# Two-layer cross-attention: layer norms in one operation, weights applied when leaving PSUM, score shift for 512 queries at once

## The chip, the cores and the metric

The kernel runs on one core of one Trainium2 chip. The metric is device time in microseconds (us) from the program's start to its end. A core has TensorE (PE in the profile, with PEld for its weight loads), VectorE (DVE), ScalarE (ACT), GpSimd (POOL) and SyncE (SP, which here only issues DMAs). They run side by side and wait for each other by semaphores. SBUF is the working memory, PSUM takes what PE computes.

## What is computed

Two batches of 512 queries (256 wide) attend to 1024 context tokens (192 wide), in two layers. In layer 0 both sides are normalised, with weights and shifts; layer 1 has eight heads, no norm in front, and ends in a norm. The norms that are changed are those of layer 0, the first of the two; layer 1's final norm is as it was.

```python
def layer_norm(x, gamma, beta):
    mu = jnp.mean(x, axis=-1, keepdims=True)
    var = jnp.mean(jnp.square(x - mu), axis=-1, keepdims=True)
    return (x - mu) * jax.lax.rsqrt(var + EPS) * gamma + beta
# layer 0
qn, kvn = layer_norm(q_feat, g_q, be_q), layer_norm(kv_feat, g_kv, be_kv)
q = qn @ Wq.T + bq ; k = kvn @ Wk.T + bk ; v = kvn @ Wv.T + bv
ctx = softmax(q @ k.T) @ v
x = q_feat + ctx @ Wd.T + bd
# layer 1: Q, K, V for 8 heads of 256, softmax(Q K^T / 16) V, @ Wo, + x, layer norm
```

## The kernel before

All matmuls take rounded fp32 operands (fp32r); each operand is split in a rounded part ("hi", written by ACT) and the remainder ("lo", written by DVE or POOL), so a product takes two or three matmuls. The weights Wq and Wk are multiplied with each other once (`absorb`, tasks T_A0 and T_A0b), so a query tile is multiplied with raw keys; likewise Wv and Wd (T_B0, T_B0b). Bias terms become two small vectors (`vec`, task T_VEC) and, for each query, one number that is added to its scores (`neg_shift`). Before softmax, DVE adds it and takes the row's minimum of the negated scores (`minimum(-1, j, 0)`, L1352), for one tile j of 128 queries after another. There is one score buffer, `ps_scores`, so PE's `scores(-1, j+1)` waits for `minimum(-1, j)`.

Every engine runs its own hand-written list of instructions in order, and that order decides everything: an instruction that waits holds all that stand behind it on its engine.

The norm of a 128-token tile went in four steps. DVE took statistics (L1470, L1478, L1481); POOL made `rstd` from the variances (L431); DVE subtracted the mean and multiplied by gamma (`ln_centre`, L1492); then, for query tiles and half of the context tiles, ACT multiplied by `rstd` (L1127) and POOL added beta (L440), and for the other half DVE did both (`ln_scale_context`, L1501). PE then transposed the tiles (`turn_chunk`, L779: two chunks of the queries, four of the context), ACT rounded them (`round_chunk`, L1142) and DVE took the remainders (`split_chunk`). The shift of the scores was a sum over each query row on DVE (`sum_shift`, L1529, four operations per batch, and `finish_shift`, L1538); its weights came from a matmul at PE's start (L792). Batch 0 goes through at once; batch 1's norm stands between batch 0's softmax steps.

Batch 0's values (`values(-1, 0, c)`, c = 0 to 3, L650 to L658) run from 46.79 us, with batch 1's context chunks turned between c = 2 and c = 3. Behind them comes `scores(-1, 4)`, the first of batch 1.

## Time and profile before

| | us |
|---|---|
| median of 3 runs (501.72 to 502.06) | 501.74 |
| the profiled execution | 501.67 |
| its span in the profile | 499.7 |
| outside the span | 1.97 |
| PE busy | 474.2 (95%) |
| DVE busy | 332.2 (66%) |
| ACT busy | 291.6 (58%) |
| POOL busy | 245.4 (49%) |

A share is the mean over stages with different limits. A row of the timeline gives start and duration; matmuls overlap, so PE's pace is the distance between their starts. The change is only in what runs in the first 60 us and in the form of the loads and stores.

### The profile page before, as it was taken

What the parts mean: (1) busy time and instruction counts of PE and PEld (TensorE: products, weight loads), DVE (VectorE), ACT (ScalarE), POOL (GpSimd) and SP (SyncE); (2) the same over time, 40 slices, a digit from 0 to 9 for tenths busy, and PEclk for the clock granted to TensorE, in tenths of its full rate; (3) what the DMA queues carried; (4) which work ended last, traced back from release to release, by engine and by line L of the source; (5) the groups of instructions that cost most, each with busy time, mean ns of one, the idle gap of its engine ahead of it and who ended that gap; (6) DMA issues with size and microseconds to landing.
All of it is one profiled execution on the core that took longest, in us unless ns stands there. A gap on an engine that the chain in (4) does not pass through costs nothing.

```text
span 499.7 us, 7565 instructions
## 1 busy us (share of the span) xinstructions
PE 474.2 (95%) x2424; PEld 395.8 (79%) x2424; DVE 332.2 (66%) x679; ACT 291.6 (58%) x482; POOL 245.4 (49%) x153
## 2 busy tenths in 40 slices
PE   0999999999999999999999999999999999999994
PEld 0877787787878888888888888888888888888893
DVE  4999866476685657565856585658565765673666
ACT  4667476467664756566666665656565655556332
POOL 4636763555855353637272717172727263454004
PEclk9999999999999999999999999999999999999998
DMA  8413013667765565665656564647473746562002
GB/s 263 147 45 127 1 29 120 212 206 227 246 214 182 177 202 176 205 211 168 210 168 210 168 214 164 226 153 238 140 244 135 252 137 220 168 210 64 0 2 84
DMA packets 53975, 81.97 MB, mean 164 GB/s; under 512 B 5793, under 2 KB 43073, under 8 KB 53825
## 3 DMA queue, kind: packets, MB, share of 16 engines
q1 hardware_dynamic: 44992, 50.16, 33.8%
q10 hardware_dynamic: 8960, 31.54, 16.8%
q8 instruction: 11, 0.18, 0.2%
q14 instruction: 12, 0.09, 0.1%
HBM read 49.16 MB, written 32.51 MB: 163 GB/s over the span
## 4 chain that ended last, share of the span: by engine, by line
PE 74%; DVE 8%; DMA 7%; ACT 4%; issue 3%; POOL 2%; SPq 1%; DVEq 0%; POOLq 0%; ACTq 0%
PE ps_scores L626 27%; PE ps_o L658 6%; PE ps_o L651 5%; PE ps_o L650 5%; PE ps_o L657 5%; PE ps_o L652 5%; DMA scratch<-probs 3%; PE ps_task L574 2%; PE ps_task L573 2%; PE ps_task L572 2%; DMA probs_t_lo<-scratch 2%; DMA ring<-in_weights_a 2%; PE ps_out L572 2%; PE ps_out L573 1%; PE ps_out L574 1%
## 5 line engine op out<-in xcount | busy, mean ns | idle before, releaser
L514 POOL TENSOR_TENSOR probs_t_lo<-probs_t_lo,probs_t_hi 128x1024 fp32r<-128x1024 f32 (+1 forms) x75 | 146.5, 1967 | 177.5 <-ACT probs_t_hi L1018 177.4
L1018 ACT ACTIVATE probs_t_hi<-probs_t_lo 128x1024 fp32r<-128x1024 f32 (+1 forms) x75 | 64.7, 881 | 37.2 <-DMA probs_t_lo<-scratch 34.7
L626 PE MATMUL ps_scores<-key_hi,q_hi 128*128 128x512 f32 x144 | 57.8, 402 | 1.3 <-DVE neg_scores L1352 0.8
L1339 DVE RECIPROCAL row_inv<-row_sum 128x1 f32<-128x1 f32 x72 | 11.3, 159 | 70.4 <-PE ps_scores L626 68.4
L650 PE MATMUL ps_o<-probs_t_hi,val_hi 128*128 128x512 f32 (+1 forms) x144 | 56.7, 393 | 1.1 <-issue 0.9
L626 PE MATMUL ps_scores<-key_rem,q_lo 128*128 128x512 f32 x144 | 56.6, 393 | 0.5 <-DVE q_lo L1434 0.3
L626 PE MATMUL ps_scores<-key_rem,q_hi 128*128 128x512 f32 x144 | 56.6, 393 | 0.0
L626 PE MATMUL ps_scores<-key_lo,q_hi 128*128 128x512 f32 x144 | 56.6, 393 | 0.0
L626 PE MATMUL ps_scores<-key_hi,q_lo 128*128 128x512 f32 x144 | 56.4, 392 | 0.0
L651 PE MATMUL ps_o<-probs_t_lo,val_hi 128*128 128x512 f32 (+1 forms) x144 | 56.3, 391 | 0.0
L658 PE MATMUL ps_o<-probs_t_lo,val_rem 128*128 128x512 f32 (+1 forms) x144 | 56.2, 392 | 0.0
L657 PE MATMUL ps_o<-probs_t_hi,val_rem 128*128 128x512 f32 (+1 forms) x144 | 55.8, 389 | 0.0
L652 PE MATMUL ps_o<-probs_t_hi,val_lo 128*128 128x512 f32 (+1 forms) x144 | 55.6, 386 | 0.0
L1376 DVE STREAM_TRANSPOSE probs<-probs 128x1024 f32<-128x1024 f32 x30 | 37.4, 1246 | 25.0 <-ACT probs L1006 24.8
L1376 DVE STREAM_TRANSPOSE neg_scores<-neg_scores 128x1024 f32<-128x1024 f32 x30 | 37.3, 1242 | 15.1 <-ACT neg_scores L1006 15.1
L444 POOL TENSOR_TENSOR w_lo<-ring,w_hi 128x1024 fp32r<-128x1024 f32 x17 | 40.9, 2408 | 6.2 <-ACT w_hi L1098 6.2
L1006 ACT ACTIVATE neg_scores<-neg_scores,row_min 128x1024 f32<-128x1024 f32 x30 | 34.5, 1148 | 13.1 <-DVE row_min L1369 13.1
L1369 DVE CUSTOM_DVE_ANT_0 probs<-ps_scores,mask_bias 128x1024 f32<-128x1024 f32 x32 | 38.9, 1216 | 3.2 <-PE ps_scores L626 3.2
L1006 ACT ACTIVATE probs<-probs,row_min 128x1024 f32<-128x1024 f32 x30 | 34.5, 1151 | 11.1 <-DVE row_min L1369 11.0
L1369 DVE CUSTOM_DVE_ANT_0 neg_scores<-ps_scores,mask_bias 128x1024 f32<-128x1024 f32 x32 | 38.8, 1213 | 0.6 <-issue 0.6
L626 PEld LDWEIGHTS ps_scores<-key_hi,q_hi 128*128 128x128 f32 x144 | 27.0, 188 | 7.5 <-DVE neg_scores L1352 2.2
L626 PEld LDWEIGHTS ps_scores<-key_rem,q_lo 128*128 128x128 f32 x144 | 27.0, 188 | 7.2 <-DVE q_lo L1434 0.6
(256 smaller groups left out, 1097.5 us busy)
## 6 DMA issues: line engine op xcount, KB each, us to landing
probs_t_lo<-scratch SPq DMA_DIRECT2D x240, 128.0 KB, 2.9
scratch<-neg_scores ACTq DMA_DIRECT2D x30, 512.0 KB, 3.1
scratch<-probs ACTq DMA_DIRECT2D x30, 512.0 KB, 3.7
ring<-in_weights_a SPq DMA_DIRECT2D x9, 512.0 KB, 5.2
ring<-in_weights_b SPq DMA_DIRECT2D x9, 512.0 KB, 5.1
ring<-in_keys_t SPq DMA_DIRECT2D x4, 512.0 KB, 3.2
ctx_raw<-in_context SPq DMA_DIRECT2D x2, 768.0 KB, 9.5
ring<-in_context SPq DMA_DIRECT2D x16, 96.0 KB, 2.6
```

Of the source, the lines that this page charges most:

```text
L444: nc.gpsimd.tensor_tensor(w_lo[:, :], ring[r][:, :], w_hi[:, :].bitcast(f32), ALU.subtract)\
L514: nc.gpsimd.tensor_tensor(pt_lo[b][:, t, k, :], pt_lo[b][:, t, k, :].bitcast(f32), moved_part(j, k).bitcast(f32), ALU.subtract).then_inc(m ...
L626: last = pe.matmul(ps_scores[:, n], left, right[:, n], start=(i == 0), stop=(i == len(passes) - 1))
L650: pe.matmul(o0, val_hi[b][:, kt, :], hi, start=(kt == 0), stop=False)
L651: pe.matmul(l0, val_hi[b][:, kt, :], lo, start=False, stop=False)
L652: pe.matmul(o0, val_lo[b][:, kt, :], hi, start=False, stop=(kt == KT - 1))
L657: pe.matmul(o1, val_rem[b][:, kt, :], hi, start=(kt == 0), stop=False)
L658: last = pe.matmul(l1, val_rem[b][:, kt, :], lo, start=False, stop=(kt == KT - 1))
L1006: act.activation(dst, src, ACT.Exp, bias=row_min[:, j:j + 1], scale=-1.0, accum_out=row_sum[:, j:j + 1]).then_inc(exped, 1)
L1018: act.activation(moved_part(j, k), pt_lo[b][:, t, k, :].bitcast(f32), ACT.Copy)\
L1369: dve.tensor_tensor_reduce(out=tiles[j % 2][:, :], in0=ps_scores[:, :], in1=mask_bias[:, b, :], scale=1.0, scalar=BIG, op0=ALU.add, op1=AL ...
L1376: dve.transpose(tiles[j % 2][:, :], tiles[j % 2][:, :]).then_inc(blocks_turned, 1)
```

## The change

- **Loads.** A partition now holds 4 neighbouring query tokens (8 context tokens) instead of every 128th, so each partition reads or writes one piece. Context of batch 0 comes in two transfers. The rows of gamma are no longer spread over 128 partitions by DMA: they come as one row each on ACT's queue and PE turns them into columns (`gains`).
- **Norm.** One operation makes `(x - mean) * rstd`: on ACT as `rstd * x + neg_means` (queries and the first context half), on DVE as a tensor_scalar (second half). DVE makes `neg_means` (`shift_means`) from POOL's `rstd`. `rsqrt` is three operations of 4 columns per batch's start instead of one of 4 and one of 8. `ln_centre`, `ln_scale_context`, `scale_tiles`, `bias_tiles` are gone.
- **Weights.** Gamma is the scale of what already leaves PSUM (`round_chunk`, `split_chunk`, `round_b`, `split_b0`).
- **Shifts.** Beta times the weight matrices is added to the biases by DVE: `fold_bias`, two sums over a row (L1575) and an addition, for bq, bk and bv.
- **Score shift.** PE multiplies the two columns `w_pair` with all 512 transposed queries (four matmuls), ACT copies the two rows out (`keep_shift`), PE turns them (`turn_shift`), DVE adds up.
- **Order.** The T_VEC matmuls stand behind all six chunks.

```diff
-            sp.dma_start(resid[:, 0:QT, :], x_tiles[:, 0:QT, :]).then_inc(x_loaded[0], 16)
-            sp.dma_start(q_rows[:, :, :], rows_q.partition_broadcast(P)).then_inc(q_rows_loaded, 16)
-            sp.dma_start(ctx_raw[:, 0:KT, :], ctx_tiles[:, 0:KT, :]).then_inc(ctx_loaded[0], 16)
-            sp.dma_start(kv_rows[:, :, :], rows_kv.partition_broadcast(P)).then_inc(kv_rows_loaded, 16)
+            sp.dma_start(resid[:, 0:QT, :], x_tiles[0]).then_inc(x_loaded[0], 16)
+            sp.dma_start(ctx_raw[:, 0:CTX_HALF, :], ctx_tiles[0, :, 0:CTX_HALF, :]).then_inc(ctx_loaded[0], 16)
+            sp.dma_start(ctx_raw[:, CTX_HALF:KT, :], ctx_tiles[0, :, CTX_HALF:KT, :]).then_inc(ctx_loaded[1], 16)
             sp.dma_start(ring[0][:, :], weights_a[0]).then_inc(ring_loaded[0], 16)
+            sp.dma_start(be_row[:, :], rows_q[1].partition_broadcast(P)).then_inc(be_row_loaded, 16)
+            sp.dma_start(kv_row[:, :], rows_kv[1].partition_broadcast(P)).then_inc(kv_row_loaded, 16)
...
+            def sum_shift(b, bank):
+                for k in range(DT):
+                    mv = slice(b * QUERIES, (b + 1) * QUERIES)
+                    pe.matmul(bank[0:2, :], w_pair[:, k, :], xt_hi[:, k, mv], start=(k == 0), stop=False)
+                    last = pe.matmul(bank[0:2, :], w_pair[:, k, :], xt_lo[:, k, mv], start=False, stop=(k == DT - 1))
+                last.then_inc(shift_rowed, 1)
...
+            def norm_tokens(b):
+                act.wait_ge(means_made, 2 * b + 1)
+                for t in range(KT, LN_TILES):
+                    n, x_tile = b * LN_TILES + t, b * QT + t - KT
+                    act.activation(xn[:, x_tile, :], resid[:, x_tile, :], ACT.Identity,
+                                   scale=rstd[:, n:n + 1], bias=neg_means[:, n:n + 1]).then_inc(x_normed, 1)
...
+            def shift_means(b, first, end, rstds):
+                n = slice(b * LN_TILES + first, b * LN_TILES + end)
+                dve.wait_ge(rstd_made, 3 * b + rstds)
+                dve.scalar_tensor_tensor(neg_means[:, n], moments[:, n, 0], -1.0, rstd[:, n], ALU.mult, ALU.mult)\
+                    .then_inc(means_made, 1)
...
             split_queries(T_Q0, 0, 0, 0)
             split_queries(T_Q0b, 0, 1, 0)
-            sum_shift(0, range(QT))
-            finish_shift(0)
+            split_chunk(0, 4)
+            split_chunk(0, 5)
+            finish_shift(0, w_bank[:, 0:2 * QT])
+            dve.wait_ge(ring_loaded[1], 16)
+            fold_bias(C_BV, ring[1], 0, kv_row, bias_v_folded)
             minimum(-1, 0, 0)
             ln_stats(1, x_token_tiles, x_loaded[1])
             ln_moments(1, KT, LN_TILES)
+            shift_means(1, KT, LN_TILES, 1)
             split_b0(T_B0, 0)
             split_b0(T_B0b, 1)
...
-            ln_centre(1, x_token_tiles)
             split_probs(-1, 0)
```

DVE between the remainders of batch 0's queries (`q_lo`) and the second minimum. Before (L1529 is the old score shift, L1352 the minimum, L1423 `split_b0`):

```order
L1434 SCALAR_TENSOR_TENSOR q_lo<-ps_task,vec,q_hi 64x512
L1529 ISA ctx_raw,neg_shift<-xn,rem_sum 128x2x128
L1529 ISA neg_shift 128x1
L1538 TENSOR_SCALAR neg_shift<-neg_shift,vec 128x4
L1352 TENSOR_SCALAR neg_scores,row_min<-ps_scores,neg_shift 128x1024
L1470 BN_STATS stats<-resid 128x6 x4
L1478 BN_AGGR moments<-stats 128x2 x4
L1481 TENSOR_SCALAR var_eps<-moments 128x4
L1423 TENSOR_TENSOR b_lo<-ps_out,b_hi 128x256
```

The same place in the changed kernel, behind the same `q_lo` row (L1505) and one more `split_chunk` row (L1600). L1603 is `split_chunk`, L1613 to L1617 `finish_shift`, L1575 and L1579 `fold_bias` for bv, L1422 the minimum, L1566 `shift_means`; `split_b0` (L1493) follows:

```order
L1603 SCALAR_TENSOR_TENSOR key_rem<-ps_turn,gains,key_rem 64x512
L1613 TENSOR_SCALAR vec<-ps_turn 128x1
L1614 TENSOR_SCALAR shift_parts<-ps_turn 128x4
L1617 SCALAR_TENSOR_TENSOR neg_shift<-shift_parts,vec,ps_turn 128x4
L1575 ISA probs,bias_parts<-ring,kv_row 128x192
L1575 ISA bias_parts 128x1
L1579 TENSOR_TENSOR bias_cols<-bias_parts,cols 128x2
L1422 TENSOR_SCALAR neg_scores,row_min<-ps_scores,neg_shift 128x1024
L1541 BN_STATS stats<-resid 128x6 x4
L1549 BN_AGGR moments<-stats 128x2 x4
L1552 TENSOR_SCALAR var_eps<-moments 128x4
L1566 SCALAR_TENSOR_TENSOR neg_means<-moments,rstd 128x4
```

Two chunk remainders and the fold of bv now stand ahead of the first minimum, and `shift_means`, which waits for POOL's `rstd`, ahead of `split_b0` and the second; the four old sums are gone. The pair of rows L1529 stands four times in the program before, the pair L1575 twice here; each is shown once.

PE from the last product of Wq and Wk to the queries. Before (L803 is T_VEC, L779 the transposes of chunks):

```order
L574 MATMUL ps_out<-w_hi,w_lo 128x256
L803 MATMUL ps_o<-cols,ring 128x1 x4
L803 MATMUL ps_o<-cols,b_full 128x1 x2
L779 MATMUL ps_scores<-ident,kvn 128x128 x4
L779 MATMUL ps_o<-ident,kvn 128x128 x4
L779 MATMUL ps_scores<-ident,kvn 128x128 x4
L779 MATMUL ps_o<-ident,kvn 128x128 x4
L572 MATMUL ps_out<-xt_hi,a_hi 128x512
```

In the changed kernel:

```order
L793 MATMUL ps_turn<-ident,kvn 128x128 x4
L840 MATMUL ps_o<-bias_cols,ring 128x1 x4
L844 MATMUL ps_o<-bias_cols,ring 128x1 x4
L800 MATMUL ps_turn<-xt_hi,w_pair 2x512
L801 MATMUL ps_turn<-xt_lo,w_pair 2x512
L800 MATMUL ps_turn<-xt_hi,w_pair 2x512
L801 MATMUL ps_turn<-xt_lo,w_pair 2x512
L584 MATMUL ps_out<-xt_hi,a_hi 128x512
```

T_VEC moved behind the chunks, and directly behind it, with only DVE's short `split_w` between, PE needs `w_pair`.

PE in batch 0's values, at c = 0 and 1 of the changed kernel (L664 to L672 are the values; before, no foreign row stands here):

```order
L672 MATMUL ps_o<-probs_t_lo,val_rem 128x512
L800 MATMUL ps_task<-xt_hi,w_pair 2x512
L801 MATMUL ps_task<-xt_lo,w_pair 2x512
L800 MATMUL ps_task<-xt_hi,w_pair 2x512
L801 MATMUL ps_task<-xt_lo,w_pair 2x512
L664 MATMUL ps_o<-probs_t_hi,val_hi 128x512
```

Four matmuls are added here, and four small transposes (L812) after c = 1.

## Rows read from the trace of the kernel before

**Rows 1.** Windows: stretch and length, busy us (instructions) of each engine, granted clock, DMA

```profile
15.00:20.00 5.00, 4.79 (x35) 4.55 (x33) 5.00 (x15) 3.71 (x10) 3.84 (x5) 1.00 0.35 101
30.00:40.00 10.00, 9.21 (x50) 7.29 (x49) 9.41 (x27) 8.60 (x18) 6.17 (x6) 1.00 0.16 53
33.10:43.60 10.50, 9.30 (x50) 7.29 (x50) 9.97 (x24) 10.41 (x20) 8.29 (x7) 1.00 0.40 142
40.00:50.00 10.00, 8.80 (x48) 6.75 (x46) 9.55 (x31) 6.73 (x14) 5.55 (x5) 1.00 0.41 158
50.00:60.00 10.00, 9.51 (x48) 7.19 (x47) 9.20 (x21) 4.57 (x11) 9.67 (x12) 1.00 0.01 2
100.00:450.00 350.00, 348.17 (x1718) 290.47 (x1717) 228.56 (x413) 213.06 (x335) 178.52 (x90) 1.00 0.61 195
```

**Rows 2.** Timeline, DVE at the start: start, us, engine, line, operation, tiles, count

```profile
4.72 1.41 DVE L1470 BATCH_NORM_STATS2 stats<-resid 128x6 f32<-128x256 f32 x4 [4.72 <-DMA resid<-in_x]
6.45 0.17 DVE L1481 TENSOR_SCALAR var_eps<-moments 128x4 f32<-128x4 f32 x1
...
12.74 1.23 DVE L1556 TENSOR_TENSOR w_lo<-ring,w_hi 128x1024 fp32r<-128x1024 f32 x1
13.88 2.71 DVE L1492 SCALAR_TENSOR_TENSOR kvn<-ctx_raw,moments,kv_rows 128x192 f32<-128x192 f32 x8
...
17.83 1.28 DVE L1509 TENSOR_TENSOR xt_lo<-ps_turn,xt_hi 128x512 fp32r<-128x512 f32 x2
...
31.35 0.22 DVE L1584 TENSOR_SCALAR mask_bias<-mask_bias 16x128 f32<-16x128 f32 x1
```

**Rows 3.** Timeline, ACT and POOL, same columns

```profile
7.82 1.71 ACT L1127 ACTIVATE xn<-xn,rstd 128x256 f32<-128x256 f32 x4 [1.16 <-POOL rstd L431]
22.95 2.39 POOL L444 TENSOR_TENSOR w_lo<-ring,w_hi 128x1024 fp32r<-128x1024 f32 x1 [2.93 <-ACT w_hi L1098]
30.37 1.02 POOL L431 TENSOR_TENSOR rstd<-var_eps,minus_half 128x4 f32<-128x4 f32 x1 [5.03 <-DVE var_eps L1481]
```

**Rows 4.** Timeline, PE from its first transposes to the first scores

```profile
13.60 1.91 PE L779 MATMUL ps_turn<-ident,xn 128*128 128x128 f32 x8
...
15.16 0.56 PE L572 MATMUL ps_task<-w_hi 128*128 128x256 f32 x1
...
16.99 0.28 PE L574 MATMUL ps_out<-w_hi,w_lo 128*128 128x256 f32 x1
...
20.94 0.48 PE L572 MATMUL ps_out<-xt_hi,a_hi 128*128 128x512 f32 x1
...
23.75 0.40 PE L626 MATMUL ps_scores<-key_hi,q_hi 128*128 128x512 f32 x1
```

**Rows 5.** Timeline, DVE from the last query remainder to the second minimum

```profile
24.68 0.74 DVE L1434 SCALAR_TENSOR_TENSOR q_lo<-ps_task,vec,q_hi 64x512 fp32r<-64x512 f32 x1 [0.36 <-ACT q_hi L1075]
...
26.38 0.41 DVE L1529 CUSTOM_DVE_ANT_0 ctx_raw<-xn,rem_sum 128x256 f32<-128x256 f32 x1
26.72 0.07 DVE L1529 DVE_READ_ACCUMULATOR2_ANT neg_shift<- 128x1 f32 x1
26.83 0.23 DVE L1538 TENSOR_SCALAR neg_shift<-neg_shift,vec 128x4 f32<-128x4 f32 x1
27.20 1.28 DVE L1352 TENSOR_SCALAR_CACHE_REDUCE neg_scores<-ps_scores,neg_shift 128x1024 f32<-128x1024 f32 x1
...
31.67 1.28 DVE L1352 TENSOR_SCALAR_CACHE_REDUCE neg_scores<-ps_scores,neg_shift 128x1024 f32<-128x1024 f32 x1
```

**Rows 6.** Timeline, PE at the second scores, and in batch 0's values

```profile
28.54 0.50 PE L626 MATMUL ps_scores<-key_hi,q_hi 128*128 128x512 f32 x1
...
46.79 0.47 PE L650 MATMUL ps_o<-probs_t_hi,val_hi 128*128 128x512 f32 x1 [0.18 <-DVE probs_t_lo L1383]
...
54.30 0.33 PE L779 MATMUL ps_scores<-ident,kvn 128*128 128x128 f32 x1 [0.27 <-DVE kvn L1501]
...
59.05 0.50 PE L626 MATMUL ps_scores<-key_hi,q_hi 128*128 128x512 f32 x1
```

More of the change, by code:

```diff
@@ L623, in scores @@
                                 pe.wait_ge(task_free, task + (1 if i == 2 else 2))
+                        if late_keys is not None and half == 1 and i in (0, 3):
+                            pe.wait_ge(chunk_split, late_keys + (1 if i == 0 else 2))
                         if keys is not None and i == 3 and half == 0:
@@ L1175, in _ @@
             round_queries(T_Q0b, 0, 1, 0)
+            round_weights(16, 1)
+            act.wait_ge(bias_v_folded, 1)
+            for k in range(DT):
+                act.activation(spread[:, DT + k, :], ones[:, :], ACT.Copy, scale=bias_cols[:, C_BV + k:C_BV + k + 1])\
+                    .then_inc(spread_made, 1)
             exp(-1, 0)
@@ L1180, in _ @@
             exp(-1, 1)
[L1181 removed]
+            norm_tokens(1)
             round_weights(32, 0)
@@ L1495, in ln_scale_context @@
-            def ln_scale_context(b):
-                dve.wait_ge(rstd_made, 2 * b + 2)
-                for t in range(CTX_HALF):
-                    n, dst = b * LN_TILES + t, kvn[b][:, t, 0:CTX]
-                    dve.wait_ge(centred, centred_no(b, t) + 1)
-                    dve.scalar_tensor_tensor(dst, dst, rstd[:, n:n + 1], kv_rows[:, 1, :], ALU.mult, ALU.add)\
-                        .then_inc(ctx_normed[0], 1)
+                    dve.tensor_scalar(kvn[b][:, t, 0:CTX], ctx_raw[:, b * KT + t, :], moments[:, n, 0:1],
+                                      rstd[:, n:n + 1], ALU.subtract, ALU.mult).then_inc(ctx_normed[1], 1)
@@ new lines, in shift_means, with fold_bias @@
+            def shift_means(b, first, end, rstds):
[3 more added lines that the diff above has]
+                    .then_inc(means_made, 1)
+            def fold_bias(side, raw, first, row, folded_by):
+                n = slice(side, side + DT)
+                width = row.shape[1]
+                for k in range(DT):
+                    spare, src = side % (2 * DT) * DIM + k * width, first + k * DIM
+                    dve.tensor_tensor_reduce(
+                        out=probs[:, spare:spare + width], in0=raw[:, src:src + width], in1=row[:, :], scale=1.0, scalar=0.0, op0=ALU.mult, op1=ALU.add,
+                        accum_out=bias_parts[:, side + k:side + k + 1]).then_inc(bias_summed, 1)
+                dve.wait_ge(bias_summed, side + DT)
+                dve.tensor_tensor(bias_cols[:, n], bias_parts[:, n], cols[:, n], ALU.add).then_inc(folded_by, 1)
@@ new lines, in finish_shift @@
+            def finish_shift(b, bank):
+                t = slice(b * QT, (b + 1) * QT)
+                sums = bank.rearrange("p (t n) -> p t n", n=2)
+                dve.wait_ge(shift_turned, b + 1)
+                if b == 0:
+                    dve.tensor_scalar(vec[:, 2:3], w_bank[:, V_CONST:V_CONST + 1], -1.0, None, ALU.mult).then_inc(shift_const, 1)
+                dve.tensor_scalar(shift_parts[:, 0:QT], sums[:, :, 0], -1.0, None, ALU.mult).then_inc(shift_summed, 1)
+                dve.wait_ge(shift_const, 1)
+                dve.wait_ge(shift_summed, b + 1)
+                dve.scalar_tensor_tensor(neg_shift[:, t], shift_parts[:, 0:QT], vec[:, 2:3], sums[:, :, 1],
+                                         ALU.add, ALU.subtract).then_inc(shift_made, 1)
```

293 lines of the change are left out of this document (165 added, 128 removed).

## The prediction

> **What bounds the kernel now.** I read the windows first. From 100 to 450 us PE is busy 348.17 of 350.00 [rows 1]: layer 1 keeps PE full and the change leaves it alone, so whatever the first 60 us gain or lose arrives unchanged at the end. In those 60 us nothing is so clear. Between 30 and 60 PE is busy 9.21, 8.80 and 9.51 of 10, DVE 9.41, 9.55 and 9.20 [rows 1]: PE and DVE hand each other work and both are nearly full. PE's idle time there, 2.5 us in all (0.79 + 1.20 + 0.49), is the most that a faster DVE could win back. ACT is a third party: from 33.10 to 43.60 it is busy 10.41 of 10.50 [rows 1]. Then I read the timeline for the points where PE is released: its first product at 15.16, the queries at 20.94, the first scores at 23.75 [rows 4], the second scores at 28.54, the values at 46.79, batch 1's first scores at 59.05 [rows 6].
>
> I go through the change by these points. D is the end of batch 0's queries, 23.75 before; M is the end of the first minimum, 27.20 + 1.29 = 28.49 before (its accumulator row included).
>
> **Part 1, up to the queries.** Removed: four DVE centrings of queries, POOL's four additions, the eight and four context operations (2.71 us for eight [rows 2]). Added: waits of DVE for POOL's rstd. Walk: x comes as long pieces; it landed at 4.72 [rows 2], I take 4.4 (bounds 4.0 and 4.7; the trace has no such load of x). Statistics to var_eps took 1.90 us (4.72 to 6.62 [rows 2]): 6.3. The first context half, 192 wide instead of 256, about 1.6: 7.9. POOL's rstd of 4 columns takes 1.02 [rows 3] plus 0.1: 9.05; neg_means and the copy of gains 0.35: 9.4. The second half 1.6: 11.0; rstd 1.1: 12.1. Four tensor_scalar norms: the nearest row in width is the scalar_tensor_tensor over 192, 2.71/8 = 0.34; the nearest in kind is L1584, 0.22 for 128 columns and one stream [rows 2]. I add 64 columns to the latter and take 0.29 (bounds 0.15 and 0.34): 13.3. w_lo takes 1.23 [rows 2]: 14.5. ACT is there in time: its four query norms (1.71 [rows 3]), four of context and w_hi end by 12.5. So PE's product starts at 14.55 instead of 15.16.
>
> PE's pace then matters. The product's twelve matmuls run from 15.16; at first they last 0.41 and start 0.21 apart, from 16.99 they last 0.28 and start 0.12 apart [rows 4]. That is 256 columns at about 1.2 and about 2.4 GHz, although the window's granted clock reads 1.00 [rows 1]. I assume that the change of pace stays near 16.8. The product ends at 17.0, three chunks (4 transposes each, 0.45) at 18.4, T_VEC's 8 matmuls (0.12 each) at 19.35. DVE meanwhile: fold bq 1.0 and bk 0.9, two remainders 1.28 [rows 2], a_lo 0.75, done at 18.45, so PE comes last. vec and split_w are four tiny operations, two of them waiting, 0.5: 19.85. The four matmuls of the shift, 512 columns at 0.23, 0.92: queries at 20.8 against 20.94. **Term 1: -0.15.** Three us of removed norm work buy almost nothing: the gain goes into three rstd waits in series, the folds, and the shift matmuls ahead of the queries. Bounds: -1.9 (x at 4.0, norms at 0.15, full pace from the first product) and +1.9 (slow pace kept, below).
>
> One page speaks on the norms. The Trainium skill (VectorE: DVE Perf Modes, "The perf-mode tier table") says that fp32 tensor_scalar inside SBUF runs two elements per cycle, where two-tensor operations run one. No row here shows such an operation at this size. By its rule the four norms would cost about 0.1 us less each, the sum 0.4 us less, an estimate from that page.
>
> **Part 2, the first minimum.** Before, q_lo of the second query half ended at D + 1.67 (24.68 + 0.74), the four sums and finish_shift at 27.06, and the minimum started at 27.20 = D + 3.45, when the scores were ready [rows 5]. The sums were hidden by the scores. Now behind q_lo: two chunk remainders (0.67 each), 1.33, to D + 3.0; finish_shift, two tiny operations and one that waits, 0.4 (L1538 ends 0.27 after the last accumulator row [rows 5]), to D + 3.4; fold of bv: one sum takes 0.34 to its accumulator (26.38 to 26.72 [rows 5]) at 256 columns, about 0.28 at 192, two of them, the accumulator 0.07 and a waiting addition 0.27, 0.9, to D + 4.3. Scores would be ready at D + 3.8: their second half now waits for those remainders. The turn_shift on PE (six small instructions, 0.7) hides under the wait for q_lo. So the minimum starts 0.9 later. **Term 2: +0.9** (bounds +0.4, where scores come last, and +1.3). PE has the product of Wv and Wd to fill in; its w_lo is split by POOL in 2.39 us [rows 3] and, since ACT's w_hi moved behind the queries, comes at D + 4.4, so the product ends at D + 5.85, at about M. It costs nothing more.
>
> **Part 3, the second minimum.** DVE then takes batch 1's statistics, and the new shift_means waits for POOL. Before, rstd ran 30.37 to 31.39 [rows 3] while DVE did split_b0 and the mask; the second minimum started at 31.67 [rows 5], M + 3.18, already later than its scores (28.54 + 2.3 + 0.2 = 31.1 [rows 6]). Now everything behind var_eps starts after rstd and neg_means (M + 2.90 + 0.2 = M + 3.1) instead of at M + 1.7. Queued behind that wait are both split_b0, the mask, the minimum, and with the minimum PE's third scores and ACT's exp. **Term 3: +1.35** (bounds +1.1 and +1.5). I see no cover: DVE had no idle time there.
>
> **Part 4, to batch 0's values.** Gone: four centrings (1.67 us on DVE at 32.88) and POOL's additions. DVE's next minimum could start 0.25 earlier, but ACT has 10.41 us of work in the 10.50 that follow [rows 1], the same instructions in the same order, and PE's transposes and DVE's remainders wait for it. **Term 4: 0** (bounds -0.4 and 0).
>
> **Part 5, values and batch 1's chunks.** From 46.79 to 59.05 are 12.26 us [rows 6]. PE's work: 40 matmuls at 0.233 are 9.32, 16 transposes at 0.115 are 1.84, together 11.2; it waited about 1.1 us, part of it for DVE's kvn ahead of 54.30 [rows 6]. Now DVE is free early (eight centrings, four scalings, four sums gone), so these waits go, but PE gets four 512-column matmuls (0.92) and four small transposes (0.45): 11.2 + 1.37 = 12.6. **Term 5: +0.35** (bounds 0 and +0.9).
>
> **Tail.** The stores are longer pieces; bounds -0.2 and 0, I take 0.
>
> **Sum:** -0.15 + 0.9 + 1.35 + 0 + 0.35 = +2.45 us on the profiled execution's 501.67 (span 499.7 and 1.97 around it): 504.1. That execution lay 0.07 below the median of the runs, so I say 504.2.
>
> **Rivals.**
> - *The slow pace lasts.* PE now transposes at about 9.9 to 12.5, idles about 2 us and starts again. If the change of pace comes only near 20, product, chunks and T_VEC run at the slow starts: 17.1, then 12 transposes at 0.22 (2.6), then 8 at about 0.2: T_VEC ends at 21.3 instead of 19.35. Total 506.1. The Trainium skill (TensorE: Matmul & The Clock Gate, "Part 1: The HAM clock gate") has the clock follow how busy PE has been recently, with the half rate as the idle state; the 0.21 against 0.12 in the trace agrees. For it: the new gap. Against: PE is active earlier as well.
> - *A better start.* x early, norms cheap, full pace at once: 504.2 - 1.9 = 502.3, within 0.2% of before.
> - *Faster than before.* DVE's queue, not ACT's or PE's, sets the pace between 30 and 59, and the 1.67 + 2.71 us of centrings and the sums give PE back most of its 2.5 us idle. That pays from the point where it outweighs terms 2 and 3, that is with a good start as well: 504.2 - 1.9 - 2.0 = 500.3. For it: DVE at 9.4 of 10. Against: ACT's full stretch, and two of the new DVE costs stand exactly where DVE was late.
> - *The loads don't get faster.* x at 4.72 instead of 4.4: 504.5, inside my forecast.
>
> **How the numbers follow.** The forecast's mechanism (503.0 to 505.6) 0.65, slow pace 0.10, better start 0.15, faster 0.10. A measurement tells 0.2% here, 1.0 us, from no change. Faster 0.10, within 0.2% 0.14, slower 0.76. The range leaves out the fast rival and the upper part of the slow one: 501.4 to 506.0.
>
> **What would show it.** Queries start at 20.4 to 21.3; first minimum at D + 4.2 or later; DVE idle for POOL's rstd ahead of neg_means in batch 1 for about 1.1 us; second minimum more than 4.3 us behind M; PE's idle time in the values nearly gone, and their stretch 12.5 us or more. I am wrong if the queries start before 19.5, if the wait for rstd is covered, or if minimum to minimum in batch 0 gets shorter by more than 0.3 us.

## The result, and the profile after

The changed kernel takes 509.48 us (median of 4 runs, 507.88 to 511.89) against 501.90 for the kernel before: a ratio of 1.0156, 95% interval 1.0126 to 1.0186. It is slower by 1.6%, 7.6 us. The forecast had the sign (504.2 us), but its range ended at 506.0. The profiled execution is the slowest of the four, 511.89 us with a span of 509.7; in what follows "offset" means how much later a point comes than in the profiled execution of the kernel before.

Windows of the kernel after (PE, PEld, DVE, ACT, POOL busy, granted clock, DMA), as [rows 1]:

```profile
15.00:20.00 5.00, 5.00 (x31) 5.00 (x30) 3.13 (x12) 2.55 (x6) 0.00 (x0) 1.00 0.02 5
20.00:25.00 5.00, 4.39 (x21) 3.29 (x21) 1.85 (x6) 1.02 (x2) 0.00 (x0) 0.74 0.31 105
25.00:30.00 5.00, 4.84 (x24) 3.72 (x23) 2.68 (x4) 2.32 (x3) 0.97 (x1) 0.92 0.00 0
30.00:40.00 10.00, 7.94 (x41) 5.83 (x41) 8.55 (x30) 4.75 (x10) 2.43 (x2) 1.00 0.06 13
40.00:50.00 10.00, 8.48 (x49) 6.79 (x47) 7.79 (x19) 10.00 (x19) 5.26 (x3) 1.00 0.41 154
50.00:60.00 10.00, 9.32 (x45) 6.63 (x45) 8.99 (x25) 3.88 (x8) 6.92 (x9) 1.00 0.12 48
100.00:450.00 350.00, 345.87 (x1704) 288.02 (x1703) 226.03 (x409) 212.57 (x333) 174.32 (x89) 1.00 0.62 195
```

DVE is relieved, as meant (8.55 and 7.79 of 10 where it had 9.41 and 9.55), and POOL too. But PE is no fuller for it (7.94 against 9.21), and in 20 to 30 us the granted clock is 0.74 and 0.92. PE's timeline shows both faults, as [rows 4] for before:

```profile
14.52 0.58 PE L584 MATMUL ps_task<-w_hi 128*128 128x256 f32 x1 [1.35 <-DVE w_lo L1641]
14.90 0.41 PE L585 MATMUL ps_task<-w_lo,w_hi 128*128 128x256 f32 x1
...
17.03 0.41 PE L586 MATMUL ps_out<-w_hi,w_lo 128*128 128x256 f32 x1
17.25 1.06 PE L793 MATMUL ps_o<-ident,kvn 128*128 128x128 f32 x4
...
19.41 0.95 PE L840 MATMUL ps_o<-bias_cols,ring 128*128 128x1 f32 x8
20.22 1.03 PE L844 MATMUL ps_o<-bias_cols,ring 128*128 128x1 f32 x8
21.86 0.39 PE L800 MATMUL ps_turn<-xt_hi,w_pair 128*2 128x512 f32 x1 [0.61 <-DVE w_pair L1587]
...
23.10 0.63 PE L584 MATMUL ps_out<-xt_hi,a_hi 128*128 128x512 f32 x1
23.53 0.63 PE L585 MATMUL ps_out<-xt_lo,a_hi 128*128 128x512 f32 x1
...
25.66 0.47 PE L584 MATMUL ps_task<-xt_hi,a_hi 128*128 128x512 f32 x1
...
27.12 0.50 PE L809 MATMUL ps_turn<-shift_parts,ones 128*128 128x1 f32 x4
...
27.89 0.50 PE L640 MATMUL ps_scores<-key_hi,q_hi 128*128 128x512 f32 x1
```

The product starts at 14.52, as forecast (14.55). All its twelve matmuls keep the slow distance of 0.21 us (the slow pace, half rate). PE is at full pace when T_VEC comes, sixteen instructions of one column each, and then waits 0.61 us. From 22.5 to 25.7 the matmuls of 512 columns (the end of the shift, then the queries) stand 0.43 apart; the granted clock is 0.50 there, 1.2 GHz again. D, the end of the queries, is 27.12 (23.75 before), and the first scores start at 27.89.

DVE's timeline after, as [rows 2] and [rows 5]:

```profile
4.66 1.41 DVE L1541 BATCH_NORM_STATS2 stats<-resid 128x6 f32<-128x256 f32 x4 [4.66 <-DMA resid<-in_x]
...
12.08 1.25 DVE L1559 TENSOR_SCALAR kvn<-ctx_raw,moments,rstd 128x192 f32<-128x192 f32 x4 [1.12 <-POOL rstd L455]
...
30.73 0.91 DVE L1575 CUSTOM_DVE_ANT_0 probs<-ring,kv_row 128x192 f32<-128x192 f32 x1
...
32.07 1.28 DVE L1422 TENSOR_SCALAR_CACHE_REDUCE neg_scores<-ps_scores,neg_shift 128x1024 f32<-128x1024 f32 x1
...
36.28 0.16 DVE L1566 SCALAR_TENSOR_TENSOR neg_means<-moments,rstd 128x4 f32<-128x4 f32 x1 [1.12 <-POOL rstd L455]
...
37.96 1.28 DVE L1422 TENSOR_SCALAR_CACHE_REDUCE neg_scores<-ps_scores,neg_shift 128x1024 f32<-128x1024 f32 x1
...
55.88 2.94 DVE L1559 TENSOR_SCALAR kvn<-ctx_raw,moments,rstd 128x192 f32<-128x192 f32 x4 [0.32 <-POOL rstd L455]
```

First minimum 32.07 (27.20 before), second 37.96 (31.67 before), with the wait for POOL's rstd ahead of it, as foreseen.

The table follows PE through all profiled executions: offset of the first, second, third and fifth scores (23.75, 28.54, 33.02 and 59.05 us before), and of PE's scores at 117 and 239 us. "Product" is the distance between its matmuls, "fall" whether the clock fell behind it.

| kernel | product | fall | 1st | 2nd | 3rd | 5th | 117 | 239 |
|---|---|---|---|---|---|---|---|---|
| after | 0.21 | yes | 4.14 | 4.88 | 6.29 | 7.53 | 7.59 | 9.99 |
| e0_same | 0.12 | yes | 1.92 | 2.65 | 4.06 | 5.31 | 5.36 | 6.98 |
| e1_vec_early | 0.12 | no | -0.24 | 0.48 | 1.90 | 3.16 | 3.53 | 2.64 |
| e2_means_late | 0.21 | yes | 3.30 | 4.02 | 4.32 | 5.56 | 5.54 | 7.06 |
| e3_fold_late | 0.21 | yes | 3.07 | 3.47 | 4.25 | 5.49 | 5.61 | 6.52 |
| e4_filler | 0.21 | no | 2.35 | 3.07 | 4.48 | 5.71 | 5.67 | 6.80 |
| e5_loads | 0.21 | no | -0.70 | -0.70 | -0.70 | -0.73 | -0.90 | -1.21 |
| e6_four_moves | 0.21 | (slow to 25.5) | 4.92 | 5.31 | 5.53 | 6.79 | 7.49 | 8.80 |
| e7_means_first | 0.12 | yes | 1.93 | 2.67 | 4.08 | 5.31 | 5.28 | 5.97 |
| e8_warm | 0.12 | no | 0.59 | 1.33 | 2.75 | 3.99 | 3.90 | 3.03 |
| e9_warm_moves | 0.12 | no | -0.21 | 0.19 | 0.39 | 1.64 | 1.58 | 0.76 |
| e10_loads_warm | 0.12 | yes | 2.97 | 2.97 | 2.96 | 2.94 | 2.92 | 2.01 |
| e11_vec_early2 | 0.21 | (slow to 24.8) | 4.73 | 5.45 | 6.86 | 8.10 | 8.44 | 10.33 |
| e12_late13 | 0.12 | no | 3.60 | 4.33 | 5.75 | 7.00 | 6.94 | 5.99 |
| e13_late6 | 0.12 | no | 2.03 | 2.76 | 4.17 | 5.40 | 5.37 | 4.42 |
| e14_warm_ab | 0.12 | no | 0.62 | 1.35 | 2.76 | 4.02 | 3.98 | 3.03 |
| e15_pool_late | 0.12 | no | 0.63 | 1.36 | 2.77 | 4.01 | 3.90 | 2.99 |

After and e0 are the same kernel: 2.2 us apart at the first scores, equal in steps from there to 117 us, and apart again in layer 1. So three things have to be explained: fixed steps of layer 0, a start that differs from run to run, and slips in layer 1 (the last column less the one ahead).

### The profile page after: what moved, and what is told of

Its sections match the earlier page's. It is cut to its first block, busy times and chain, and to the rows that moved or that the text cites. A ratio compares the mean times of both kernels' runs of the same rounds, so it can differ in the third digit from the quotient of the medians.

```text
span 509.7 us, 7585 instructions
## 1 busy us (share of the span) xinstructions
PE 480.6 (94%) x2448; PEld 400.1 (78%) x2448; DVE 326.1 (64%) x666; ACT 295.4 (58%) x483; POOL 231.8 (45%) x139
## 4 chain that ended last, share of the span: by engine, by line
PE 76%; DVE 8%; ACT 5%; DMA 5%; issue 3%; POOL 2%; SPq 0%; DVEq 0%; POOLq 0%; ACTq 0%
PE ps_scores L640 26%; PE ps_o L664 6%; PE ps_o L672 6%; PE ps_o L665 6%; PE ps_o L671 6%; PE ps_o L666 6%; PE ps_task L584 2%; PE ps_task L586 2%; PE ps_task L585 2%; DMA scratch<-probs 2%; DMA probs_t_lo<-scratch 2%; PE ps_out L584 2%; ACT probs L1057 2%; PE ps_out L585 2%; PE ps_out L586 1%
## 5 line engine op out<-in xcount | busy, mean ns | idle before, releaser
L664 PE MATMUL ps_o<-probs_t_hi,val_hi 128*128 128x512 f32 (+1 forms) x144 | 56.9, 395 | 2.9 <-DVE o_lo L1461 1.9
L672 PE MATMUL ps_o<-probs_t_lo,val_rem 128*128 128x512 f32 (+1 forms) x144 | 56.3, 392 | 0.0
L664 PEld LDWEIGHTS ps_o<-probs_t_hi,val_hi 128*128 128x128 f32 x144 | 27.2, 189 | 8.6 <-DVE o_lo L1461 2.2
```

The costliest lines, as they stand in the source:

```text
L664: pe.matmul(o0, val_hi[b][:, kt, :], hi, start=(kt == 0), stop=False)
L672: last = pe.matmul(l1, val_rem[b][:, kt, :], lo, start=False, stop=(kt == KT - 1))
```

## Experiments: the steps of layer 0

The first theory: the forecast's steps are real and add up, and the start has lost something more. The rival: the steps replace each other, so undoing one gives nothing. A medians' difference under 2 us says little here, since four runs of one kernel differ by 2 to 9 us; the steps in the table differ by 0.01 us between after and e0.

**e0_same**: the changed kernel once more.

> The changed kernel again, as the ruler for its neighbours and to see what of it varies. Its profiled run of 511.89 us had three parts over the kernel before: +7.5 us by the first scores of batch 1, and two late steps in layer 1 (+0.8 near 196 us, +1.6 near 222 us). If all of this belongs to the change, every run lies near 510 to 512. If the clock's fall during batch 0's queries (1.2 us) and the layer 1 steps are chance, some runs lie at 508 and their profile lacks one of them.

510.54 us (508.73 to 512.51), ratio 1.0202 (1.0167 to 1.0237). Its profile showed that the start isn't a fixed loss.

**e1_vec_early** and **e11_vec_early2**, the same edit, profiled twice:

```diff
             last.then_inc(task_done, 1)
+            for c in range(X_CHUNKS + 1, CHUNKS):
+                turn_chunk(0, c)
             pe.wait_ge(chunk_split, X_CHUNKS)
```

(and the same loop taken out ahead of T_VEC).

> The changed kernel with the T_VEC matmuls put back ahead of chunks 3 to 5, as in the kernel before; nothing else. Theory A (the wait for w_pair and the clock's fall come from T_VEC and DVE's split_w standing alone in front of the queries): the 0.6 us wait goes, TensorE keeps its pace, the queries end 1.5 to 2.2 us earlier, total 1.5 to 2 us below the changed kernel. Rival (the clock falls because of the gap before the first product, whatever stands there later): only the wait goes, total 0.5 to 0.7 us below.

> The same kernel as e1, for a second profile: e1's was of its fastest run, 504.5 us, where the clock did not fall; its others took 510.2 to 513.7. Theory: a profile of 508 us or more shows PE's slow pace at the product, the queries, or both, with the first scores 2 to 5 us later than in the kernel before. Rival (the spread is made in layer 1): first scores as in e1 (0.2 us sooner than before), and 4 us or more of waits added behind 110 us.

Medians 510.8 (504.47 to 513.73) and 510.85 (504.81 to 512.45). One code, two profiles: 504.47 us with PE at full rate through the whole start and first scores 0.24 us *sooner* than before; 512.45 with the slow pace from 14.5 to 24.8 us and first scores 4.73 later. The order of T_VEC isn't what decides; PE's pace is.

**e2_means_late**: `shift_means` for batch 1's tokens behind the second minimum.

```diff
-            shift_means(1, KT, LN_TILES, 1)
             split_b0(T_B0, 0)
...
             minimum(-1, 1, 0)
+            shift_means(1, KT, LN_TILES, 1)
```

> The changed kernel with batch 1's first shift_means put behind the second minimum, so DVE doesn't wait for POOL's rstd ahead of split_b0. Theory (the wait lies bare on the path): the second minimum starts about 3.2 us behind the end of the first instead of 4.6, total 1.3 us below the changed kernel. Rival (ACT's full stretch behind takes it back): under 0.4 us.

508.93 us (507.62 to 509.49). From second to third scores the offset grows by 0.30 instead of 1.41: term 3 is this wait.

**e3_fold_late**: the fold of the value bias behind batch 1's statistics instead of ahead of the first minimum (ACT's copies that need it move too).

```diff
-            dve.wait_ge(ring_loaded[1], 16)
-            fold_bias(C_BV, ring[1], 0, kv_row, bias_v_folded)
             minimum(-1, 0, 0)
...
             ln_moments(1, KT, LN_TILES)
+            dve.wait_ge(ring_loaded[1], 16)
+            fold_bias(C_BV, ring[1], 0, kv_row, bias_v_folded)
```

> The changed kernel with the fold of bv taken from ahead of the first minimum and put into the gap in which DVE waits for POOL's rstd in batch 1 (its spare output goes to another tile, ACT's two spreads stand behind round_b). Theory: the first minimum starts when the scores are ready, about D + 3.9 instead of D + 4.95, the fold hides in the wait of 1.1 us: total 0.9 to 1.1 us below the changed kernel. Rival (PE's product of Wv and Wd, which waits for POOL's w_lo until D + 4.4 and ends at D + 5.9, comes last then): only 0.3 us.

508.09 us (506.23 to 508.74). DVE's timeline of e3:

```profile
30.00 1.28 DVE L1422 TENSOR_SCALAR_CACHE_REDUCE neg_scores<-ps_scores,neg_shift 128x1024 f32<-128x1024 f32 x1 [0.24 <-PE ps_scores L640]
...
33.00 0.35 DVE L1576 CUSTOM_DVE_ANT_0 ctx_raw<-ring,kv_row 128x192 f32<-128x192 f32 x1
```

The first minimum now waits for the scores; first to second scores cost 0.40 instead of 0.73, second to third 0.78 instead of 1.41, because the fold now fills part of the wait for rstd: 0.97 us in all, where 0.9 to 1.1 was expected. In its old place the first sum took 0.91, beside POOL's split of w_lo; here it takes 0.35.

**e7_means_first** (one edit, `shift_means(1, 0, CTX_HALF, 2)` ahead of `norm_context(1)`):

> The changed kernel with batch 1's shift_means for the first half of the context ahead of norm_context on DVE, so that ACT's norms don't wait for DVE's. Theory: the values' stretch (fourth to fifth scores) that grew by 1.24 us grows by 0.5 to 0.9 instead. Rival (the stretch is bound by DVE's own norms of 2.94 us, which POOL's adds of the residual slow): it stays at 1.2 or more. Time 508 to 511 us either way, since 0.5 us is less than the runs of this kernel differ.

508.41 us (506.82 to 510.94). Fourth to fifth scores: +1.19 (4.12 to 5.31), against 1.25 in e0. The rival held, but its reason was still untested. **e15_pool_late** tested it, on top of e8 (below):

```diff
             pool.wait_ge(outb_made, 1)
+            pool.wait_ge(chunk_split, 2 * CHUNKS)
             for t in range(BATCHES * QT):
```

> The kernel of e8 with POOL's eight adds of the residual (0.74 us each, 5.7 us in all, beside DVE's norms of batch 1's context) held back until batch 1's chunks are split; POOL was idle for 12 us behind them. Theory (the adds slow DVE: four norms took 2.94 us there and 1.25 in batch 0): the norms take 1.2 to 1.8 us, the stretch from the fourth to the fifth scores grows by 0.3 to 0.7 us against the kernel before in place of 1.24, time 504.0 to 504.4 us. Rival (the norms aren't what PE waits for, or the adds meet other DVE work later): the stretch stays, or the time is 504.8 us or more.

504.78 us (504.73 to 505.04), as e8. Its DVE timeline, and its PE timeline in the values:

```profile
52.36 1.25 DVE L1568 TENSOR_SCALAR kvn<-ctx_raw,moments,rstd 128x192 f32<-128x192 f32 x4 [0.32 <-POOL rstd L455]
```

```profile
52.09 0.40 PE L673 MATMUL ps_o<-probs_t_lo,val_rem 128*128 128x512 f32 x1
52.32 0.39 PE L801 MATMUL ps_task<-xt_hi,w_pair 128*2 128x512 f32 x1
...
53.25 0.39 PE L665 MATMUL ps_o<-probs_t_hi,val_hi 128*128 128x512 f32 x1
...
55.35 0.40 PE L673 MATMUL ps_o<-probs_t_lo,val_rem 128*128 128x512 f32 x1
...
56.01 0.50 PE L665 MATMUL ps_o<-probs_t_hi,val_hi 128*128 128x512 f32 x1
```

The norms fall from 2.94 to 1.25 us, so POOL's adds did slow them, and PE starts its fifth scores not a bit sooner (+4.01): nobody on the path waited for them. PE itself is the bound: it has 0.93 us of shift matmuls (52.32 to 53.25) and 0.43 of their transposes (0.66 from 55.35 to 56.01, where 0.23 is the rule) more to do. The Trainium skill (GPSIMD Engine Reference, "1. Specifications") has GpSimd share its way to SBUF with VectorE; the pairs 2.94/1.25 and 0.91/0.35 agree.

## Experiments: the pace of PE

The second theory: PE's pace at the start follows from what PE did just ahead, and the change made PE idle there. Before, matmuls of 256 columns and the transposes ran from 11.8 us into the product without a gap; now PE idles 3.2 us ahead of its first transposes, 1.4 us ahead of the product, and has T_VEC's tiny columns and a wait of 0.6 us ahead of the shift. The rival: it comes and goes with the run, whatever PE does.

**e4_filler**: four dummy products between T_VEC and the shift.

```diff
+            pe.wait_ge(task_free, 2)
+            for n in range(4):
+                pe.matmul(ps_task[:, :], w_hi[:, 0:P], w_hi[:, 0:BANK], start=(n == 0), stop=(n == 3))
             pe.wait_ge(chunk_split, X_CHUNKS)
             pe.wait_ge(w_split, 1)
             sum_shift(0, w_bank)
```

> The changed kernel with four dummy products of 512 columns on PE between task T_VEC and sum_shift, in which PE otherwise waits for w_pair; nothing else differs, and the results of the dummies are overwritten. Theory (clock): the granted clock fell to 0.50 for some 3.4 us in four of five profiles because PE had only one-column products and a wait there. Then the dummies keep the clock at 1.00 in 20 to 25 us, and the first scores start 0 to 2.4 us later than in the kernel before (instead of 1.9 to 4.1), although the dummies themselves take 0.9 us where 0.6 was waited; time 506 to 508 us. Rival (the fall is chance, or comes from what PE did ahead of T_VEC): the clock falls again, the first scores start 2.2 to 4.4 us later and the time is 509 to 511 us.

508.6 us (504.94 to 509.31). No fall in its profile, but the slow pace held at the product up to 18 us, and the median is above the 506 to 508 us of the theory. Half the cure.

**e6_four_moves**: the edits of e1, e2, e3 and e7 together.

> The changed kernel with four pieces moved together: the two context chunks behind T_VEC and not ahead of it (as in e1), shift_means behind the second minimum (as in e2), the fold of the value bias behind the second batch's statistics (as in e3), and batch 1's shift_means for the context ahead of norm_context. Theory (the losses of layer 0 are separate waits that add): with the clock at 1.00 the first scores start within 0.3 us of the kernel before, the third 0.5 to 1.0 later, the fifth 1.5 to 2.2 later; with one fall of the clock 2 us more. Time 503 to 506 us. Rival (a wait that goes is replaced by the next one): the third scores still start over 3 us later than the first ones do against the kernel before, and the time is 508 us or more.

509.01 us (508.14 to 510.53). This looked like a refutation of the steps, and wasn't: PE ran at the slow pace from its first product on,

```profile
14.34 0.58 PE L584 MATMUL ps_task<-w_hi 128*128 128x256 f32 x1 [1.35 <-DVE w_lo L1641]
...
25.07 0.63 PE L585 MATMUL ps_out<-xt_lo,a_hi 128*128 128x512 f32 x1
25.49 0.48 PE L586 MATMUL ps_out<-xt_hi,a_lo 128*128 128x512 f32 x1
```

until 25.5 us. Its first scores come 5.1 us later than those of the same order at full pace (e9, below); from there to the third the offset grows by 0.61, not 2.15.

**e8_warm**: e4 and dummy transposes in the two idle times ahead of the product.

```diff
             last.then_inc(gains_turned, 1)
+            pe.wait_ge(ones_set, 1)
+            for n in range(15):
+                pe.transpose(ps_task[:, 0:P], ones[:, :], ident[:, :])
...
+            for n in range(6):
+                pe.transpose(ps_task[:, 0:P], ones[:, :], ident[:, :])
             pe.wait_ge(piece_split, PC_A0 + 1)
             absorb(T_A0, 0)
```

> The changed kernel with PE kept at work in its idle times before the queries: 15 dummy transposes (0.20 us each at the slow pace) behind the gains' transposes, where PE waits 3.2 us for the first normed tiles, 6 more where it waits 1.4 us for w_lo, and the four dummy products of e4. Theory (PE's pace at the start follows from what PE did just ahead): the 12 products of w_hi and w_lo at 14.3 us run at 0.12 us each from the first or soon after it, as in two of the nine profiles so far, and the clock doesn't fall between 19 and 26 us; the first scores start 0 to 1.0 us later than in the kernel before, and all four runs lie within 2 us of each other, median 505 to 507 us. Rival (the pace comes and goes by chance of the run, whatever PE does): some of the products still run at 0.21 us, first scores 2 us or more later, median 508 us or more.

504.79 us, and all four runs between 504.77 and 504.81; ratio to before 1.0072 (1.0047 to 1.0097). PE's timeline of e8:

```profile
14.33 0.39 PE L584 MATMUL ps_task<-w_hi 128*128 128x256 f32 x1 [1.16 <-DVE w_lo L1649]
14.55 0.28 PE L585 MATMUL ps_task<-w_lo,w_hi 128*128 128x256 f32 x1
...
20.86 0.39 PE L584 MATMUL ps_out<-xt_hi,a_hi 128*128 128x512 f32 x1
...
23.58 0.50 PE L809 MATMUL ps_turn<-shift_parts,ones 128*128 128x1 f32 x4
...
24.34 0.50 PE L640 MATMUL ps_scores<-key_hi,q_hi 128*128 128x512 f32 x1
```

Work whose results nobody reads takes 4.7 us off the changed kernel and a spread of 4 us with it. The rival has fallen: the pace does follow what PE did. But not all of the 4.7 us is pace. In the two profiles 3.7 us of the difference are there at 117 us, and the rest arises in layer 1, for another reason (below).

**e14_warm_ab**: e8 without the four dummy products.

> The kernel of e8 without the four dummy products between T_VEC and the sum of the shift, so that only PE's idle times ahead of the product are filled. Theory (the fall of the clock belongs to the one-column products of T_VEC and the 0.6 us wait behind them): the product runs at 0.12 us each from 14.3 us, and the clock falls near 19.5 us as in e0, first scores 1.9 to 2.4 us later than in the kernel before, time 508 to 510 us. Rival (work done earlier is what keeps it): no fall, first scores 0.3 us later, time 504.5 us.

505.93 us (504.76, 505.76, 506.10, 506.21). The profile is of the fastest and shows no fall; the others are 1.0 to 1.4 us slower. So work ahead of the product does most of it, and my claim that T_VEC and the wait behind it make the fall alone is refuted. Whether they are what slows the other three runs isn't shown: those have no profile.

**e9_warm_moves**: e6 with e8's dummy transposes.

> The kernel of e6 (four pieces moved) with the dummy transposes of e8 ahead of the product, without the four dummy products. In e6 PE ran at the slow pace from 14.3 to 25.5 us, which hid what the moves were worth. Theory (pace and waits are separate and add): first scores within 0.5 us of the kernel before, third 0.6 later than that, fifth 1.5 to 2.2 later than the kernel before; median 502 to 505 us. Rival (the moves are worth nothing, only the clock matters): median as e8's or above.

502.50 us (nine of ten runs 502.41 to 503.31; one took 598.6 us, for a reason that nothing here shows); ratio 1.0024 (1.0013 to 1.0035). Against e8 the moves are worth 2.3 us once the pace is held, where e6 showed nothing. Pace and waits are separate and add (in the profiles 2.35 us at the fifth scores, 3.99 less 1.64).

**e5_loads**: the one part of the change that stands alone, on the kernel before.

```diff
-    x_tiles = x.rearrange("(t p) d -> p t d", p=P)
+    x_tiles = x.rearrange("(b p t) d -> b p t d", p=P, t=QT)
```

(and `out`, `context` and their DMAs in the same way).

> The kernel before with one part of the change alone: tokens dealt to partitions in stretches, for the loads of x and context and the stores. My prediction put the gain at 0.1 to 0.4 us of the first load, which PE's start (bounded by the weights' split) may not pass on: time within 0.5 us of the kernel before. Rival (the new layout is slower, for the loads, the stores or layer 1): the time is 1 us or more above it, and the slips in layer 1 come with it.

499.89 us (499.58 to 500.38, 7 runs) against 500.93: ratio 0.9970 (0.9955 to 0.9984). Better than both kernels. DVE's timeline of e5 and of before:

```profile
4.21 1.41 DVE L1470 BATCH_NORM_STATS2 stats<-resid 128x6 f32<-128x256 f32 x4 [4.21 <-DMA resid<-in_x]
...
8.90 2.18 DVE L1470 BATCH_NORM_STATS2 stats<-ctx_raw 128x6 f32<-128x192 f32 x8 [0.75 <-DMA ctx_raw<-in_context]
```

```profile
9.84 2.17 DVE L1470 BATCH_NORM_STATS2 stats<-ctx_raw 128x6 f32<-128x192 f32 x8 [1.15 <-DMA ctx_raw<-in_context]
```

x comes 0.51 us sooner (4.72 in [rows 2]) and the context 0.94, and 0.70 of it reaches the first scores. I had looked at x alone.

**e10_loads_warm**: e5 with 20 dummy transposes at PE's start.

> The kernel before with the loads and stores in stretches (e5) and 20 dummy transposes at PE's start, where it waits for the first weights until 10.8 us. Theory of the pace: the 12 products that ran at 0.21 us from 14.2 to 16.9 us in e5 run at 0.12 us, about 1 us sooner; DVE's remainders of the chunks (16.88) are then what the next steps wait for, so the first scores start 0.7 to 1.3 us before those of the kernel before (e5: 0.7); median 499.2 to 499.9 us. Rival (dummies change nothing, or take the clock down later): 500 us or more.

502.32 us (500.66 to 505.15), worse than e5. PE's timeline:

```profile
14.01 0.28 PE L573 MATMUL ps_task<-w_lo,w_hi 128*128 128x256 f32 x1
...
18.40 0.66 PE L779 MATMUL ps_scores<-ident,kvn 128*128 128x128 f32 x4 [1.69 <-DVE kvn L1505]
...
22.06 0.63 PE L573 MATMUL ps_out<-xt_lo,a_hi 128*128 128x512 f32 x1
22.49 0.63 PE L574 MATMUL ps_out<-xt_hi,a_lo 128*128 128x512 f32 x1
```

The product is fast, so PE is done early, idles 1.69 us for DVE (and 0.80 us again at 20.75), and the clock falls just ahead of the queries, for 6.8 us. In e5, with the slow product, PE has no such idle time and the clock doesn't fall. Speeding PE up where DVE is the bound bought an idle time; that the idle time cost the clock agrees with e8, but rests on one profile of each.

## Experiments: the slips in layer 1

From 117 to 239 us the offset grew by 0.7 to 2.4 us in eight profiles, all with a late start, and shrank by 0.9 in e1, e8 and e9. Lateness was the obvious suspect: something in layer 1 that keeps its own time. **e12_late13** and **e13_late6** are e8 with 17 and 10 dummy products for 4:

```diff
-            for n in range(4):
-                pe.matmul(ps_task[:, :], w_hi[:, 0:P], w_hi[:, 0:BANK], start=(n == 0), stop=(n == 3))
+            for n in range(17):
+                pe.matmul(ps_task[:, :], w_hi[:, 0:P], w_hi[:, 0:BANK], start=(n == 0), stop=(n == 16))
```

> The kernel of e8 with 17 dummy products of 512 columns ahead of the sum of the shift in place of 4: at 0.23 us each this pushes the queries and all that follows back by 3.0 us at full clock. Layer 0's offset at 117 us, 3.9 us in e8, is then 6.9, as in the changed kernel (7.6). Theory (layer 1's slip belongs to lateness, because something in it keeps its own time): between 165 and 227 us it loses 0.7 to 2.4 us where e8 gained 0.9, so the time is 509.4 to 511.1 us. Rival (the slip belongs to the fall of the clock, or to chance): it gains 0.9 us as e8 did and the time is 507.8 us.

> As e12 with 10 dummy products in place of 4, so 1.4 us later than e8 and some 5.3 us behind the kernel before at 117 us, where e0, e2, e3, e4 and e7 stood. Theory (lateness): layer 1 loses 0.7 us or more, time 507.9 to 509.0 us. Rival: 506.2 us.

507.79 us (507.71 to 507.84) and 506.20 (506.06 to 506.25): the rival's numbers, 507.8 and 506.2. Both gain 0.95 in layer 1, about as e8 does (0.9). Lateness is out. e13 and e0 make good twins, 5.37 and 5.36 late at 117 us; ACT's timeline of e13, then of e0:

```profile
182.46 0.33 ACTq L1086 DMA_DIRECT2D scratch<-probs  x1
...
190.71 1.15 ACT L1077 ACTIVATE probs_t_hi<-probs_t_lo 128x512 fp32r<-128x512 f32 x2 [2.20 <-DMA probs_t_lo<-scratch]
```

```profile
182.50 0.33 ACTq L1078 DMA_DIRECT2D scratch<-probs  x1
...
192.54 1.15 ACT L1069 ACTIVATE probs_t_hi<-probs_t_lo 128x512 fp32r<-128x512 f32 x2 [3.99 <-DMA probs_t_lo<-scratch]
```

The spill of probs to memory (ACT's queue writes the tile out, SP's reads it back in four pieces) is issued at the same time to 0.04 us, and its return lets ACT go on 1.8 us later in e0. ACT's work stands behind that wait, DVE's remainders behind ACT's, and PE waits at 201 us for `b_lo`, 0.69 us in e0 and not at all in e13:

```profile
201.03 0.38 PE L584 MATMUL ps_out<-b_hi,o_hi 128*128 128x256 f32 x1 [0.69 <-DVE b_lo L1519]
```

The same happens again near 219 us, where ACT waits 4.43 us in e0 and PE then 1.15. That is how the slip is made, and this one wait of ACT sorts all profiles: 1.7 to 2.9 us where layer 1 gained 0.8 to 1.0 (e1, e8, e9, e10, e12 to e15), 3.1 where it gained 0.3 (e5), 3.6 to 5.1 where it lost 0.7 to 2.4 (the other eight). The kernel before, against which all this is counted, waits 3.5 us, and its PE 0.41 for `b_lo`, so a kernel without that wait gains on it:

```profile
195.43 0.38 PE L572 MATMUL ps_out<-b_hi,o_hi 128*128 128x256 f32 x1 [0.41 <-DVE b_lo L1448]
```

Where does the return lose its time? The DMA records of the two traces tell. The return is issued as soon as the spill has landed, and the spill landed 3.72 us behind its issue in e13 and 4.93 us in e0; the return then took 4.50 and 5.08. In e0 one packet of the queue that the profile's page lists as "instruction" (16 KB of program being fetched) starts at 183.68 and takes 1.23 us. Of the spill's 128 packets of 4 KB, 120 start by 185.35; the last eight, as many as one of the 16 DMA engines has to carry, start one after another up to 186.80. In e13 there is no such fetch between 178.2 and 202.5 us, and all 128 have started by 185.49. This sorts the profiles without an exception: in the eight that lost time in layer 1 a fetch starts 0.8 to 2.0 us behind the issue of this spill, which then takes 4.7 to 5.6 us; in the other nine, and in the kernel before, none starts between its issue and its landing, and it takes 2.9 to 3.8 us. Each of layer 1's 60 spills can be compared with itself over the 18 traces: for 14 of them some traces have such a fetch and others none, and in all 14 the spill takes longer on average with it, by 0.2 to 1.6 us.

From 100 to 230 us such a fetch comes with every 200 to 290 records of PE's matmuls and weight loads, so I take them for fetches of PE's program. Then dummy instructions at the start must pull the later ones forward, and they do. Less each kernel's offset at 117 us, the fetch in question starts at 178.4 us in after, 178.3 in e0, 178.1 in e4 (4 dummies), 174.7 in e14 (21), 172.7 in e8 (25), 171.6 in e13 (31) and 170.7 in e12 (38), against a spill from 177.1 on. So the dummies did two things. They kept PE's pace, and by an accident of counting they moved a fetch off a spill that PE waits for; e10, whose clock fell and which gained 0.91 all the same, belongs to the same order. In e1, without dummies, the fetch comes just behind the spill (180.7), and in e11, the same code, in the midst of it (178.5); why it came 2.2 us later in e1 stays open.

## Why the prediction was wrong

- **The whole.** With PE's pace held (e8) the changed kernel takes 504.79 us, inside the 503.0 to 505.6 that the forecast's mechanism was given. That the whole lands there is in part luck: its steps (3.99 us at the fifth scores) are 1.5 us above the forecast sum of 2.45, and layer 1 gives 0.9 back. The other 4.7 us of the measured 509.48 are the start's pace and the slips in layer 1. In the profiled execution: 3.99 us of steps (e8's fifth scores), 3.55 of pace (4.14 less 0.59), 2.40 in layer 1, and 0.2 outside the span, of 10.22.
- **Term 1 (-0.15) is the step that failed**, by its sentence "I assume that the change of pace stays near 16.8", and by having no term at all for a second fall. The walk itself was good: product 14.52 for 14.55, and in e8 the queries start at 20.86, 0.08 sooner than before, within the range named (20.4 to 21.3); in the run after they start at 23.10. Its parts were off in ways that cancel: x landed at 4.66, not 4.4; the four DVE norms took 1.25 us where I had 1.16 (the 0.4 us less of the estimate beside it didn't come); T_VEC's eight matmuls are 16 instructions on PE, 1.8 us, where I had 8 and 1.0; the product at full pace makes up for both (and e8 has its four dummy products of 0.23 us where the 0.6 us wait was). The rival "the slow pace lasts" named the right mechanism and got 0.10 and 1.9 us. It had PE's new gap in it, and took PE's earlier activity for as good as steady work. It wasn't: the transposes end at 13 us and the product starts 1.35 us of idleness later.
- **"Whatever the first 60 us gain or lose arrives unchanged at the end"** failed too. PE was counted as full from 100 to 450 us, and it was, but its few waits there hang on the spills: layer 1 added 2.40 us in after and 1.62 in e0, and gave 0.9 back in e8.
- **Term 2 (+0.9)** measured +1.49: the first minimum starts at D + 4.94 in e8 (28.52 with D at 23.58) and D + 4.95 in after, for D + 4.3. The missing 0.6 is the first fold sum, 0.91 for 0.28, beside POOL's split. The `turn_shift` "hides under the wait for q_lo": it didn't ahead of the scores, 0.76 us from 23.58 to 24.34, but the first minimum wasn't waiting for scores, so it cost nothing more.
- **Term 3 (+1.35)** measured +1.42 (second minimum at M + 4.61 in e8, 4.60 in after; idle for rstd 1.12). Right, and e2 shows the cause.
- **Term 4 (0)** was right to the third minimum and short by 0.36 to the values. The cause is in ACT's rows: four norms with scale and bias take 2.07 us where four with a scale took 1.70, and ACT was the bound there. Before, then after:

```profile
34.21 1.70 ACT L1127 ACTIVATE xn<-xn,rstd 128x256 f32<-128x256 f32 x4
```

```profile
40.50 2.07 ACT L1177 ACTIVATE xn<-resid,neg_means,rstd 128x256 f32<-128x256 f32 x4
```

- **Term 5 (+0.35)** measured +0.88. I credited PE with 1.1 us of idleness to win back, from a sum of mean durations; the window of before over that stretch has PE busy 11.77 of 12.26 us, so only 0.49 was there. The added 1.37 us of matmuls were sized rightly (1.36 measured).
- **Tail and loads.** On the kernel before, long pieces are worth 1.04 us (e5), more than the 0.3 that I took for x (0.0 to 0.7) and the 0 to 0.2 for the stores. In the changed kernel x came only 0.06 us sooner (4.66 for 4.72); why not the 0.51 of e5, no run shows.
- **The rival "faster than before"** took DVE's near-full windows for the bound. DVE got its relief and PE became no fuller.
